# One layer of gated recurrence and FFN on one core: biases added by transfers, fc2 tiles held back, scales turned on TensorE

## The reference, cut to what matters

```
pre = layernorm(x) @ W + b;  i, f, o, z = split(pre)          # W: 256 x 1024
i = 10*tanh((i + input_bias)/10);  f = -softplus(f);  o = sigmoid(o);  z = tanh(z)
m' = max(f + m, i);  c = exp(f+m-m')*c + exp(i-m')*z;  n = exp(f+m-m')*n + exp(i-m')   # step by step
h = o * c/(n + 1e-6);   x1 = x + h/rms(h) * scale
w1 = (fc1_q - 128) * fc1_scales (one scale per 128 rows and column);  w2 alike
y = silu((layernorm(x1)*gamma + beta) @ w1 + b1);   out = x1 + 0.5*(y @ w2 + b2)
```

## Time and profile before

| what | value |
|---|---|
| median of 3 runs | 310.28 us |
| the profiled execution | 311.77 us, its span 310.0 us |
| TensorE busy | 294.7 us (95%), 1728 matmuls |
| VectorE busy | 269.5 us (87%) |
| ScalarE busy | 229.7 us (74%) |
| GpSimd busy | 126.4 us (41%) |
| chain that ended last | PE 39%, DVE 38%, issue 11%, ACT 5%, POOL 5%, DMA 2% |

### The profile page before, as it was taken

The page is one execution under the profiler, slowest core; times in us unless marked ns, Lnnn a source line. Parts: engine busy times, 40 slices in busy tenths (PEclk is TensorE's granted clock), DMA queues, the critical chain, the costliest instruction groups (busy, mean ns, idle before and its releaser), DMA issues.

```text
span 310.0 us, 4767 instructions
## 1 busy us (share of the span) xinstructions
PE 294.7 (95%) x1728; PEld 256.3 (83%) x1728; DVE 269.5 (87%) x487; ACT 229.7 (74%) x370; POOL 126.4 (41%) x131
## 2 busy tenths in 40 slices
PE   7999999979899899999999999999999799988996
PEld 5778789856897789988897889987898699868896
DVE  3998989999899999999999997999999987692741
ACT  2699987889879966899876978599866983921720
POOL 3043058300290529512970179012992198155000
PEclk9999999899999999999999999999999979999999
DMA  7980021060000030012000300020000011000201
GB/s 266 349 304 0 0 44 27 0 135 2 0 1 2 34 101 5 0 66 71 1 2 34 102 2 0 0 71 1 0 2 34 3 33 68 2 0 2 70 0 68
DMA packets 11127, 14.73 MB, mean 48 GB/s; under 512 B 720, under 2 KB 10208, under 8 KB 10848
## 3 DMA queue, kind: packets, MB, share of 16 engines
q1 hardware_dynamic: 10368, 12.07, 11.3%
q0 software_dynamic: 320, 1.58, 2.6%
q10 hardware_dynamic: 416, 0.79, 0.7%
HBM read 8.67 MB, written 4.19 MB: 42 GB/s over the span
## 4 chain that ended last, share of the span: by engine, by line
PE 39%; DVE 38%; issue 11%; ACT 5%; POOL 5%; DMA 2%; DVEq 0%; POOLq 0%; ACTq 0%
PE z_ps L236 5%; PE z_ps L237 4%; PE z_ps L238 4%; DVE y_lo L854 4%; PE mm_ps L236 4%; PE mm_ps L237 4%; PE mm_ps L238 4%; DVE rec L763 3%; DVE rec L756 3%; DVE rec L778 3%; DVE g L822 3%; DVE bn L835 3%; PE mm_ps L329 2%; PE mm_ps L322 2%; DVE rows L830 2%
## 5 line engine op out<-in xcount | busy, mean ns | idle before, releaser
L236 PE MATMUL z_ps<-w_hi,y_hi 128*128 128x256 f32 x248 | 71.8, 290 | 2.6 <-DVE rows L891 1.9
L237 PE MATMUL z_ps<-w_lo,y_hi 128*128 128x256 f32 x248 | 70.9, 286 | 0.0
L238 PE MATMUL z_ps<-w_hi,y_lo 128*128 128x256 f32 x248 | 70.8, 286 | 0.0
L573 ACT ACTIVATE y<-mm_ps,b_all,unit 128x512 f32<-128x512 f32 x54 | 41.6, 770 | 12.8 <-PE mm_ps L329 12.8
L236 PEld LDWEIGHTS z_ps<-w_hi,y_hi 128*128 128x128 f32 x248 | 47.6, 192 | 3.8 <-DVE rows L891 2.1
L237 PEld LDWEIGHTS z_ps<-w_lo,y_hi 128*128 128x128 f32 x248 | 47.6, 192 | 0.3
L238 PEld LDWEIGHTS z_ps<-w_hi,y_lo 128*128 128x128 f32 x248 | 47.6, 192 | 0.0
L322 PE MATMUL mm_ps<-gt_hi,w_hi 128*128 128x512 f32 x124 | 39.9, 403 | 1.6 <-ACT y L573 1.6
L854 DVE TENSOR_TENSOR y_lo<-y,y_hi 128x512 fp32r<-128x512 f32 x56 | 37.6, 687 | 4.0 <-ACT y_hi L576 3.7
L236 PE MATMUL mm_ps<-xt_hi,wg_hi 128*128 128x512 f32 x96 | 38.4, 400 | 1.1 <-ACT f_gate L505 1.1
L329 PE MATMUL mm_ps<-gt_lo,w_hi 128*128 128x512 f32 x124 | 38.8, 394 | 0.0
(11 more groups left out here) (179 smaller groups left out, 665.2 us busy)
## 6 DMA issues: line engine op xcount, KB each, us to landing
out<-rows SPq DMA_DIRECT2D x15, 256.0 KB, 2.1
rows<-x SPq DMA_DIRECT2D x7, 512.0 KB, 6.5
q<-fc_q SPq DMA_DIRECT2D x2, 1024.0 KB, 10.8
wg_raw<-fc_scales SPq DMA_DIRECT2D x1, 1024.0 KB, 7.1
w_lo<-q POOLq DMA_DIRECT2D x1, 1024.0 KB, 7.0
wg_raw<-w_gates SPq DMA_DIRECT2D x1, 512.0 KB, 5.7
wg_raw<-w_gates ACTq DMA_DIRECT2D x1, 512.0 KB, 6.0
w_lo<-q POOLq DMA_DIRECT2D x1, 512.0 KB, 4.6
```

The source lines that it names most:

```text
L236: pe.matmul(dst, wh[w_at], ah[a_at], start=start, stop=False)
L237: pe.matmul(dst, wh[w_at], al[a_at], start=False, stop=False)
L238: return pe.matmul(dst, wl[w_at], ah[a_at], start=False, stop=stop)
L573: act.activation(y[:, j % YBUFS], fc1_bank(c, j), ACT.Silu, bias=b1_all[:, j:j + 1], scale=unit[:, j:j + 1]).then_inc(silu_done, 1)
```

## The change

- **Bias by transfers.** `base_bias` is gone from VectorE. At the end of `base(c)` GpSimd waits for its own 4 steps and issues an accumulating transfer of half of b2, repeated 4 times, onto the 512 KB of rows. `final` and `last_final` wait for that transfer (`biased`, now one semaphore for even and one for odd chunks).
- **Scales as rows.** fc1's scales come as 16 rows of 128, TensorE turns them after 8 of the 16 idle products, VectorE copies them out.
- **The low part of w2** is one VectorE subtraction (128x2048) after `input_times_z(2)`.
- **High parts of y** all on ScalarE: chunk 0's tiles 4 to 7, chunk 6's 6 and 7, and the odd ones of chunk 7.
- **Chunk 3's gates** come in another order (`Z_SOONER`), with two of them taken before chunk 0's last high parts.
- **Chunk 0's fc2** takes the low part of w2 last for its first two tiles (`fc2_first`).
- **The end.** `h_turned(7)` comes after 5 tiles of fc1(6) instead of 2. The last row tile of fc2(5) and of fc2(6) is held back: behind fc1(6) tile 5, and behind fc1(7). `final(5, 0)` stands before `newton(7)`, `final(5, 1)` behind `ln2(7)`, `final(4, 1)` before `divisor(7)`. `g_normalised(7)` goes from GpSimd to ScalarE; ScalarE takes `g_high(6)` before `reciprocal(7)`. Chunk 6's y lies in other buffers (`y_high_of`, `y_low_of`).

```diff
@@ TensorE
             pe.wait_ge(zeros_ready, 1)
-            idle_passes(IDLE_PASSES)
+            idle_passes(IDLE_PASSES // 2)
             pe.wait_ge(ident_ready, 2)
+            pe.wait_ge(s1_in, 16)
+            pe.transpose(mm_ps[:, 0, 0:KD * KF], s1_rows[:], ident[0:KD * KF, 0:KD * KF]).then_inc(s1_turned, 1)
+            idle_passes(IDLE_PASSES // 2)
...
+            def fc2_first():
+                first = [slice(n * P, n * P + P) for n in (0, 2)]
+                pe.wait_ge(silu_done, at(0, 8, 6))
+                pe.wait_ge(w2_rounded, 2)
+                for k in range(KF):
+                    pe.wait_ge(y_lo_done, k + 1)
+                    for u in range(2):
+                        pe.matmul(z_ps[:, u, 0], y_hi[:, k, first[u]], w2_hi[:, k], start=(k == 0), stop=False)
+                        pe.matmul(z_ps[:, u, 0], y_lo[:, k, first[u]], w2_hi[:, k], start=False, stop=False)
+                pe.wait_ge(w2_ready, 1)
+                for u in range(2):
+                    for k in range(KF):
+                        pe.matmul(z_ps[:, u, 0], y_hi[:, k, first[u]], w2_lo[:, k], start=False, stop=(k == KF - 1))
...
             gates(3, range(2, GJ))
-            fc2(0, range(0, 3))
+            fc2_first()
+            fc2(0, [1])
             g_turned(1)
-            fc2(0, range(3, TT))
+            fc2(0, [3])
             fc1(1, range(0, 2))
             x_turned(4)
-            fc1(1, range(2, 5))
+            fc1(1, range(2, 6))
             h_turned(2)
-            fc1(1, range(5, KF))
+            fc1(1, range(6, KF))
...
-            fc2_both(5, 0)
+            fc2_both(5)
             g_turned(6)
-            fc2_both(5, 1)
-            fc1(6, range(0, 2))
+            fc2(5, [1])
+            fc1(6, range(0, 5))
             h_turned(7)
-            fc1(6, range(2, KF))
-            fc2_both(6, 0)
+            fc1(6, range(5, 6))
+            fc2(5, [3])
+            fc1(6, range(6, KF))
+            fc2_both(6)
             g_turned(7)
-            fc2_both(6, 1)
+            fc2(6, [1])
             fc1(7, range(KF))
+            fc2(6, [3])
             fc2(7, range(TT))
@@ ScalarE
-            silu(0, range(0, 4))
+            silu_alone(0, range(0, 2))
+            for j in range(2):
+                act.wait_ge(silu_done, at(0, 8, j + 1))
+                act.activation(y_hi[:, j], y[:, j], ACT.Copy).then_inc(y_hi_done, 1)
+            silu(0, range(2, 4))
             silu_alone(0, range(4, KF))
             square_sums(1)
+            gates(3, range(2, 4))
+            for j in range(4, KF):
+                act.wait_ge(silu_done, at(0, 8, j + 1))
+                act.activation(y_hi[:, j], y[:, j % YBUFS], ACT.Copy).then_inc(y_hi_done, 1)
             act.preload_act_table_set("sigmoid_and_others")
-            gates(3, range(2, GJ))
+            gates(3, range(4, GJ))
...
             g_normalised(6)
+            g_high(6)
             act.preload_act_table_set("natural_log_exp_and_others")
             reciprocal(7)
-            g_high(6)
...
-            silu(6, range(2, 6))
-            silu_alone(6, range(6, KF))
+            silu(6, range(2, KF))
+            g_normalised(7)
             g_high(7)
-            for j in range(0, KF, 2):
-                silu(7, range(j, j + 1))
-                silu_alone(7, range(j + 1, j + 2))
+            silu(7, range(KF))
@@ VectorE
             def final(c, u):
                 b = c % XBUFS
                 dve.wait_ge(fc2_done, at(c, 2, u + 1))
-                dve.wait_ge(biased, c + 1)
+                dve.wait_ge(biased[c % 2], at(c // 2, 16, 16))
...
-            dve.wait_ge(s1_in, 16)
+            dve.wait_ge(s1_turned, 1)
+            dve.tensor_copy(s1[:].rearrange("p k j -> p (k j)"), mm_ps[:, 0, 0:KD * KF]).then_inc(s1_out, 1)
...
-            y_low(0, range(0, 1))
+            y_low(0, range(0, 4))
             input_times_z(2)
-            y_low(0, range(1, 2))
-            y_low(0, range(2, 4))
-            for j in range(4, KF):
-                y_high(0, j)
-                y_low(0, range(j, j + 1))
+            dve.wait_ge(w2_rounded, 2)
+            dve.tensor_tensor(w2_lo[:], w2_f, w2_hi[:].bitcast(F32), ALU.subtract).then_inc(w2_ready, 1)
             mean_square(1)
             h_scaled(1)
+            y_low(0, range(4, 6))
             residual(1)
+            y_low(0, range(6, 7))
             ln2_sums(1)
+            y_low(0, range(7, KF))
             ln2(1)
...
-            base_bias(4)
             denominators(7, range(KD))
             final(4, 0)
             mean_square(6)
+            final(4, 1)
             divisor(7)
...
-            final(4, 1)
             y_low(5, range(5, KF))
             numerators(7)
             o_times_c(7)
+            g_low(6)
+            final(5, 0)
             newton(7)
             refined(7)
-            g_low(6)
             h(7)
-            base_bias(5)
-            final(5, 0)
-            final(5, 1)
             y_low(6, range(0, 2))
             mean_square(7)
-            y_low(6, range(2, 3))
             h_scaled(7)
             residual(7)
-            y_low(6, range(3, 4))
+            y_low(6, range(2, 4))
             ln2_sums(7)
-            y_low(6, range(4, 5))
             ln2(7)
-            y_low(6, range(5, 6))
-            for j in range(6, KF):
-                y_high(6, j)
-                y_low(6, range(j, j + 1))
-            base_bias(6)
+            final(5, 1)
+            y_low(6, range(4, KF))
             g_low(7)
             final(6, 0)
+            y_low(7, range(KF))
             final(6, 1)
-            base_bias(7)
-            for j in range(KF):
-                y_split_last(j)
@@ GpSimd, at the end of base(c)
+                pool.wait_ge(base_done, at(c, 4, 4))
+                pool.wait_ge(b2_halved, 1)
+                pool.dma_start(rows[:, b], b2_bc[:].unsqueeze(1).to_broadcast([P, TT, D]), accum_op=ALU.add
+                               ).then_inc(biased[c % 2], 16)
...
-            pool.dma_start(s1[:], fc1_scale_cols).then_inc(s1_in, 16)
+            pool.dma_start(s1_rows[:], fc1_scales.rearrange("k (j c) -> (k j) c", c=P)).then_inc(s1_in, 16)
...
-            pool.wait_ge(w2_rounded, 2)
-            negated(w2_lo[:], w2_hi[:], w2_negated)
-            whole_added(w2_lo[:], w2_f, w2_negated, w2_ready)
...
-            g_normalised(7)
             base(7)
```

More of the change, by code:

```diff
@@ L41, in at, with tile_of, layer @@
     return per * c + k
+def tile_of(c, j):
+    return Z_SOONER[j] if c == 3 else j
 def exists(c):
     return 0 <= c < CHUNKS
-def layer(nc, x, w_gates, cols, scale_row, fc1_q, fc1_scale_cols, fc2_q, fc2_scales, b2_row, out):
+def layer(nc, x, w_gates, cols, scale_row, fc1_q, fc1_scales, fc2_q, fc2_scales, b2_row, out):
     x_view = x.rearrange("s (c t p) d -> s c p t d", t=TT, p=P)
@@ L160, in xt, with y_high_of, y_low_of @@
             return [y_hi[:, 0:KD], y_lo[:, 0:KD]] if c == 1 else [xt_hi[:], xt_lo[:]]
+        def y_high_of(c, j):
+            if c != CHUNKS - 2:
+                return y_hi[:, j]
+            return (wg_hi if j < 4 else wg_lo)[:, j % 4 // 2, j % 2 * T:j % 2 * T + T]
+        def y_low_of(c, j):
+            if c != CHUNKS - 2:
+                return y_lo[:, j]
+            if j < 4:
+                return (xt_hi if j < 2 else xt_lo)[:, j % 2]
+            return y_more[:, j - 4]
         ident_ready, half_ready, zeros_ready = sem("ident_ready"), sem("half_ready"), sem("zeros_ready")
@@ L188, in layer @@
         ln2_stat, ln2_r, g_done = sem("ln2_stat"), sem("ln2_r"), sem("g_done")
-        base_r, base_done, biased = sem("base_r"), sem("base_done"), sem("biased")
+        base_r, base_done = sem("base_r"), sem("base_done")
+        biased = [sem(f"biased{u}") for u in range(2)]
         gt_ready, gt_hi_done, gt_lo_done = sem("gt_ready"), sem("gt_hi_done"), sem("gt_lo_done")
         fc1_done, silu_done = sem("fc1_done"), sem("silu_done")
-        y_hi_done, y_lo_done, y_hi_own = sem("y_hi_done"), sem("y_lo_done"), sem("y_hi_own")
+        y_hi_done, y_lo_done = sem("y_hi_done"), sem("y_lo_done")
         fc2_done, final_done = sem("fc2_done"), sem("final_done")
@@ L330, in fc1, with fc2_block @@
                     ins.then_inc(fc1_done, 1)
+            def fc2_block(c, n, k):
+                dst, rows_of = fc2_out(c, n), slice(n * P, n * P + P)
+                hi, lo = y_high_of(c, k)[:, rows_of], y_low_of(c, k)[:, rows_of]
+                pe.matmul(dst, hi, w2_hi[:, k], start=(k == 0), stop=False)
+                pe.matmul(dst, hi, w2_lo[:, k], start=False, stop=False)
+                return pe.matmul(dst, lo, w2_hi[:, k], start=False, stop=(k == KF - 1))
             def fc2(c, tiles):
@@ L643, in _ @@
             x_high(4)
-            silu(1, range(2, 5))
+            silu(1, range(2, 6))
             square_sums(2)
-            silu(1, range(5, KF))
+            silu(1, range(6, KF))
             act.preload_act_table_set("sigmoid_and_others")
@@ L748, in maximum @@
```

(12 more changed lines are left out.)

74 lines of the change are left out of this document (26 added, 48 removed).

## The result

The changed kernel takes **318.84 us** (median of 4 runs, 317.44 to 321.35), the kernel before 309.91 beside it: a ratio of 1.029, 95% interval 1.021 to 1.038. That is slower by 2.9%, and above the forecast's range of 307.0 to 318.0. The executions of the changed kernel spread over 4 us, and the profiled one is among the two short ones. The profiled execution took 317.58 us (span 315.8), 5.8 more than that of before. Part 1 of its page, against the earlier trace rows: VectorE has lost 13 us of work, TensorE has 2 us more and waits longer.

A forecast was written before the change was run, and what follows sets the result against it. TensorE, busy 294.7 of 310.0 us, was taken as the bound, so only its gaps could be won. Start +1.2, middle 0 and end +2.5 gave +3.7: 315.5 profiled, 314.0 for the median, range 307.0 to 318.0.

The forecast's parts named there:

- The step that failed: Chunks 1 to 3: `base` ends over 4 us before VectorE comes to `final`, so the transfer is hidden within 1 us.
- Middle: Stretch to 168 us: shorter waits of TensorE are given back by delays elsewhere; 0 taken, ends -2.5 and +1.5 us.
- Bias by transfer: GpSimd's 512 KB accumulating transfer: 4.6 us from issue to landing, hidden except for chunks 4 and 5.
- The end: Tail: late biases delay `h_turned(7)` by 3.1 us, plus 0.1 behind it; +2.5 taken, ends -2.8 and +4.7 us.
- The gap of 4 us before `fc2_both(6)`: Tail: TensorE waits there 4 us for `final(5, 1)`, which stands behind `ln2(7)`; before it was 2.9.
- a hoped pace of GpSimd: Tail: base steps at the short pace of 0.56 us would end base(5) 2.0 us sooner; set against the computed delay.
- Start: Scales land at 7.2 us, then 8 more idle products delay `spread`; +1.2 us taken, ends -1 and +4.
- the upper bound: Start: with the clock low, the second eight idle products take twice as long, +2.5 us, +4 at worst.
- From trace to median: Whole kernel: the profiled execution before was 1.49 us above its median, so the forecast is brought down by that.
- B: Rival for the whole time: late bias, but GpSimd's four steps take 2.2 us; 310.5 us, 307.2 to 313.3, chance 0.27.
- C: Rival for the whole time: bias lands before VectorE wants it; 305.8 us, 303 to 307.1, chance 0.23.
- held-back tiles do not fill the gap: Tail: the gap before `fc2_both(6)` is 4 us with or without the held-back tiles put in it.

The follow-up runs named there:

- run 5: Changed kernel with the finals of chunks 1 to 3 alone put later in VectorE's order, transfers kept: 313.57 us, ratio 1.010 to the kernel before.
- run 4: Changed kernel with the finals of chunks 0 to 5 all put later in VectorE's order, transfers kept: 307.57 us, ratio 0.991 to the kernel before.
- run 10: Changed kernel with bias transfers of a quarter of the bytes, the other row tiles' half of b2 missing: 308.95 us, ratio 0.994 to the kernel before.
- run 12: The changed kernel measured again, with no edit: 320.03 us, ratio 1.028 to the kernel before.
- run 2: Changed kernel without any bias, neither transfer nor add, half of b2 missing in the output: 309.22 us, ratio 0.996 to the kernel before.
- run 9: Changed kernel with unread matmuls put into TensorE's waits ahead of `h_turned(4)` and `h_turned(7)`: 317.56 us, ratio 1.023 to the kernel before.
- run 13: Kernel with all finals later, with scales as columns again and the 16 idle products in one row: 306.86 us, ratio 0.987 to the kernel before.
- run 14: The kernel of run 13 with `h_turned(3)` behind three tiles of fc1(2) instead of two: 305.53 us, ratio 0.984 to the kernel before.
- run 1: Changed kernel with the bias added by VectorE again, all other edits kept: 309.64 us, ratio 0.999 to the kernel before.
- run 8: Changed kernel with VectorE's adds for the bias and the old tail, early edits kept: 310.61 us, ratio 1.000 to the kernel before.

## Why the forecast was wrong

- **The step that failed** is "In chunks 1 to 3 `base` ends over 4 us before VectorE comes to `final`, within 1 us; hidden". In the trace of before `base(2)` ended at 161.0, and VectorE came to `final(2, 0)` only at 165.8, which is over 4 us. But in front of that `final` stood the add that the change removes. VectorE was free for it at 164.46, by GpSimd's and VectorE's timelines:

```profile
153.88 7.13 POOL L1183 TENSOR_SCALAR rows<-rows,up,nr 128x256 f32<-128x256 f32 x4
```
```profile
164.46 1.21 DVE L877 TENSOR_TENSOR rows<-rows,b_bc 128x1024 f32<-128x1024 f32 x1
```
  That is 3.45 us for a landing of 4.6: 1.15 short by the forecast's own price (for chunks 1 and 3 it was 4.75 and 5.20). In the changed kernel VectorE, relieved by the early edits, came 0.97 sooner, `base(2)` ended 0.47 later, and from there to the landing it was 5.5 us and not 4.6: 1.15 + 0.97 + 0.47 + 0.9 = 3.5, the wait that the trace has. I rounded three chunks into one sentence, counted an add that is gone, and held VectorE's arrival still while moving everything else. It made +3.2 at `h_turned(4)` (against the kernel with all finals later) and +1.4 of clock behind it; run 5 gives 5.3 for it by the medians.
- **Middle, 0 taken:** `h_turned(4)` is at -2.0 without the late bias (run 4) and at +1.2 with it, and behind the low clock it is +2.6, above my upper end of +1.5. The early edits won 2.5 us by `g_turned(2)`, the lower end; half of that went into `h_turned(3)`, where VectorE was next.
- **Bias by transfer, 4.6 us taken:** it was 5.2, and 0.3 before the issue. The Trainium skill (DMA: Bandwidth & Descriptors, Anatomy of one DMA — SWDGE (gpsimd) path) gives 2.0 us and the bytes over 436 GB/s, an estimate of 3.2 us for 512 KB. The first part agrees with the 1.9 us of run 10; the whole does not, since the eight transfers took 5.1 to 5.5 us.
- **The end, +3.2 computed, +2.5 taken:** +3.3 from `h_turned(6)` on. The mechanism was as told: VectorE stands at `final(4, 0)` for 3.2 us and at `final(5, 0)` for 6.3 (told 2 and 5), and `h_turned(7)` comes behind h(7), 3.7 later than before when counted from `h_turned(6)` (told 3.1). The gap of 4 us before `fc2_both(6)` shows as 0.55 in this trace, because TensorE ran at 1.2 GHz up to it. It is 1.9 in run 12, with half as much low clock, and 2.7 in runs 2 and 9, with none before it. Lowering the computed sum by a hoped pace of GpSimd was wrong: base(5) did take 3.2 and not 4.2 us, but came later, with all else.
- **Start, +1.2 taken:** the scales land as told, and `spread` starts at 9.05 (told 9.2); `x_turned(2)` then starts 0.15 later than before in the first trace. Over all, its mean is 34.8 us in the 12 traces with rows and 33.8 in the 4 with columns: +1.0, near what was taken, and by the slow second eight that were named for the upper bound.
- **From trace to median:** 1.49 us were taken off, as before's traced run was high. The changed kernel's was 1.3 us low: 5.8 + 1.5 + 1.3 = 8.6, the loss against the 310.28 of the forecast. Its idle products behind the pause ran at full pace, and in run 12's trace, of an execution of 320.59 us, they did not. That fits; with two traces it is not shown to be the whole reason.
- **The sum of it.** The median is 4.8 us over the forecast of 314.0: +2.4 from the middle, +0.8 from the end, -1.05 from the start in the profiled execution, and 2.75 from trace to median. By the traces alone the loss is 5.8 us, which put on 310.28 gives 316.1, inside the range: the early edits gained 2 us more by `h_turned(4)` than was taken, and hid part of the failed step.
- **Rivals.** B fell: GpSimd's fast steps did not come soon enough. C's time (303 to 307.1) is reached in runs 13 and 14, by order and not by speed. That held-back tiles do not fill the gap before `fc2_both(6)` agrees with runs 1, 2 and 9, where it is 2.7 us with them in place; that the new tail as a whole is worth nothing is not shown (run 8).

Left open: why the stretch of low clock at 53 us lasts 3.4 us in some traces, 6.8 in others, with rows and with columns, and is missing in three; and which of the early edits won the 2.5 us, since none was run alone.

## What to carry to other kernels

Before an add becomes a transfer, take from the trace, for every iteration by itself, the time between the producer's end and the consumer's arrival. Take the removed add out of that arrival, and move it by what the rest of the change gives it. A wait in an in-order queue is paid by all that stands behind it. If the consumer is not urgent, put it behind what is: here the same transfers cost 9 us against the adds in one order and nothing in another. Look also at what the relieved engine was worth: 10.7 us less work on VectorE bought nothing.

## What was not expected of the hardware

- The accumulating transfer of 512 KB took 5.2 us, that of 128 KB 2.7 us (a line through the two: 1.9 us and 157 GB/s), and two of 256 KB took 3.7 us each with 1.2 us of GpSimd's issue for each.
- Behind a pause of 1.5 to 2.2 us, eight idle products ran at less than full pace in 8 of 12 traces, and in 5 the granted clock fell. With 16 in one row the second eight were slow (2.6 and 3.1 us) in 2 of 4 traces, and the granted clock fell in none before 51 us.
- A low clock inside a stretch that another wait ends costs nothing (the tail in runs 9 and 12); one in a full stretch cost 1.4 us in 3.4.
